# Routed experts: results go to token order by indirect stores inside the tile loop, and come back by plain loads

## The reference, cut to what matters

```
shared = geglu(xf, w1s, w2s, w3s)            # 128 -> 512 -> 128
logits = xf @ Wg                             # 8 experts
idx = argmax(logits, axis=-1)
for e in range(8):
    y = geglu(xf, W1[e], W2[e], W3[e])
    final = final + where(idx == e, y, 0)
x = x + shared + final                       # xf is the normed x
```

## Time and profile before

| | us |
|---|---|
| median of 3 runs | 2236.22 |
| the runs | 2234.86 to 2237.25 |
| span of the profiled execution | 2237.5 |
| the part of the last stage from its first instruction to the start of the routed loop | 1998.7 to 2068.7 |
| routed loop | 2068.7 to 2181.8 |
| last two shared blocks on PE | 2181.8 to 2202.9 |
| after PE's last product | 2202.9 to 2237.5 |

### The profile page before, as it was taken

How to read it: one execution, slowest core, us unless ns; L and a number is a source line. 1 busy time by engine, 2 the same in 40 slices (tenths; PEclk the granted TensorE clock), 3 DMA queues, 4 the chain that set the end, 5 groups by cost and what they waited for, 6 DMA issues and landing times. The chain is left out here.

```text
span 2237.5 us, 80353 instructions
## 1 busy us (share of the span) xinstructions
PE 2061.6 (92%) x27341; PEld 1519.6 (68%) x27342; DVE 1563.5 (70%) x5619; ACT 1272.5 (57%) x3620; POOL 1097.6 (49%) x1151
## 2 busy tenths in 40 slices
PE   7899999988999899988999999999789999989993
PEld 5577777765767677766777777777456666665992
DVE  6878888865777743347999899989666666653542
ACT  5555565556888433336777777777545555532330
POOL 2233434434888200007777777777266666615115
PEclk9999999998999899998999999999899999979997
DMA  6610000000000000001111111111310000001112
GB/s 217 201 64 0 0 0 0 0 1 1 0 0 0 1 1 0 0 9 43 37 35 35 35 35 41 41 35 57 124 53 0 0 0 0 0 2 43 46 41 77
DMA packets 42521, 71.61 MB, mean 32 GB/s; under 512 B 6336, under 2 KB 30912, under 8 KB 41792
## 3 DMA queue, kind: packets, MB, share of 16 engines
q1 hardware_dynamic: 39104, 63.63, 9.0%
q0 software_dynamic: 3328, 6.82, 0.9%
HBM read 61.00 MB, written 9.44 MB: 31 GB/s over the span
## 5 line engine op out<-in xcount | busy, mean ns | idle before, releaser
L2334 ACT ACTIVATE xat_scores<-xat_scores,xat_least 128x257 f32<-128x257 f32 x512 | 258.5, 505 | 83.8 <-DVE xat_least L2475 83.6
L2475 DVE CUSTOM_DVE_ANT_0 xat_scores<-bank,xat_mask_b 128x257 f32<-128x257 f32 x512 | 203.1, 420 | 51.5 <-PE bank L2180 44.9
L1111 POOL TENSOR_TENSOR gqa_rnorm<-gqa_norm_min,gqa_minus_half 128x12 f32<-128x12 f32 x64 | 145.8, 2278 | 103.7 <-DVE gqa_norm_min L1188 103.7
L2236 PE MATMUL bank<-ident,xat_scores 128*128 128x128 f32 x1024 | 189.5, 288 | 0.2 <-DVE xat_p_T L2482 0.2
L751 POOL TENSOR_TENSOR lin_q_softmax<-lin_q_exp,lin_q_rsum 128x512 f32<-128x512 f32 x64 | 66.7, 1042 | 225.2 <-DVE lin_q_rsum L812 225.2
L2236 PEld LDWEIGHTS bank<-ident,xat_scores 128*128 128x128 f32 x1024 | 116.0, 141 | 81.9 <-issue 43.6
L1754 DVE SCALAR_TENSOR_TENSOR X<-bank,expert_shares,X 128x128 f32 (+1 forms) x256 | 72.2, 344 | 130.7 <-PE bank L1668 130.4
L1691 ACT ACTIVATE moe_gelu<-bank 128x512 f32<-128x512 f32 x128 | 76.4, 598 | 146.0 <-PE bank L1658 146.0
L1429 POOL TENSOR_TENSOR bat_scores<-bat_scores,bat_max 128x512 f32<-128x512 f32 x128 | 130.4, 1041 | 32.6 <-DVE bat_max L1461 32.6
L1668 PEld LDWEIGHTS bank<-moe_w,moe_gelu 128*128 128x128 f32 x1024 | 124.2, 192 | 30.8 <-issue 18.4
L1461 DVE CUSTOM_DVE_ANT_0 bat_scores<-bank,bat_causal_add 128x128 f32<-128x128 f32 x512 | 110.7, 286 | 47.0 <-PE bank L1317 47.0
(11 more groups left out here) (325 smaller groups left out, 5891.7 us busy)
## 6 DMA issues: line engine op xcount, KB each, us to landing
glu_ctx_N<-in_ctxN SPq DMA_DIRECT2D x32, 576.0 KB, 3.7
xat_ctx_T<-in_ctxT SPq DMA_DIRECT2D x32, 516.0 KB, 3.6
xat_pad<-in_xat_pad SPq DMA_DIRECT2D x32, 128.5 KB, 3.3
expert_w<-in_glx_w SPq DMA_DIRECT2D x1, 4096.0 KB, 14.6
slot_rows<-gqa_zero_rows SPq DMA_DIRECT2D x1, 2560.0 KB, 11.0
slt_rows<-slot_rows SPq DMA_DIRECT2D x40, 64.0 KB, 1.8
slot_results<-slt_y POOLq DMA_DIRECT2D x40, 64.0 KB, 1.8
moe_w<-in_moe_w SPq DMA_DIRECT2D x2, 1024.0 KB, 5.9
```

Of the source, the lines that this page charges most:

```text
L1111: pool.tensor_tensor(rn[h][:, :], sm[h][:, :], half_neg[:, :], ALU.pow).then_inc(rnorm, 1)
L2236: m = pe.transpose(dst[:, c * P:(c + 1) * P], sx[j % 2][:, g, c * P:(c + 1) * P], k.ident[:, :])
L2334: act.activation(sx[j % 2][:, g, :], sx[j % 2][:, g, :], ACT.Exp, bias=mn[j % 2][g][:, 0:1], scale=-1.0, accum_out=sm[j % 2][:, g:g + 1]). ...
L2475: dve.tensor_tensor_reduce(sx[j % 2][:, g, :], pS[g][:, 0:J], mb[slot][:, j, :], 1.0, BIG, ALU.add, ALU.min, mn[j % 2][g][:, 0:1]).then_in ...
```

## The change

- Each normed row in DRAM gets a 129th word that holds the token's number as an unsigned integer. POOL copies the numbers of all tokens into the last column of `k.XN`; the rows of `slot_rows` are 129 words (516 bytes) now, and so are the scatters and the tile loads. The numbers (`token_numbers`, partition times 32 plus tile) are a new input, loaded with the other weights of the last stage.
- `slot_rows` is no longer filled from a tile of zeros: SP copies it from a new input in DRAM (`empty_rows`), whose rows are zeros and a number beyond 4095, a different one for each slot. POOL's `memset` of the zero tile goes.
- In the routed loop POOL's store of `yo` becomes an indirect store to the row that the 129th word of `xr` names, in a buffer `token_results` of 4096 + 5120 rows. An empty slot's row goes to its own row behind the tokens.
- `xr` must keep the numbers until that store is done. So SP waits for the store before it reloads the buffer, and there are 6 buffers in place of 4.
- The 32 gathers are gone. SP waits for the last stores and issues five plain loads (L1839 of the changed kernel) into a new tile `res`, 4096 or 2048 bytes for each partition.
- DVE adds the first four groups behind the four gates of the last shared block, and only the fifth behind the last add of the shared layer. The output stores follow as before.

```diff
-    WAYS = 4
+    WAYS = 6
...
+            def again(before, t, w, stores):
+                sp.wait_ge(turned, before + 1)
+                sp.wait_ge(stored[w % 2], stores)
+                load(t, w)
+            TURNS = ST // WAYS - 1
+            with sp.Fori(0, TURNS) as i:
                 for w in range(WAYS):
-                    sp.wait_ge(turned, WAYS * i + w + 1)
-                    load(WAYS * i + w + WAYS, w)
+                    again(WAYS * i + w, WAYS * i + w + WAYS, w, 16 * (WAYS // 2 * i + w // 2 + 1))
+            for t in range(WAYS * (TURNS + 1), ST):
+                again(t - WAYS, t, t % WAYS, 16 * ((t - WAYS) // 2 + 1))
+            for w in range(2):
+                sp.wait_ge(stored[w], 8 * ST)
+            of_tokens = results[0:NT * P, :].rearrange("(p t) d -> p t d", t=NT)
+            for g, (lo, hi) in enumerate(GROUPS):
+                sp.dma_start(res[:, lo:hi, :], of_tokens[:, lo:hi, :]).then_inc(gathered[g], 16)
...
+            pool.tensor_copy(k.XN[:, :, D:D + 1].bitcast(U32), tokens[:, :].unsqueeze(2)).then_inc(numbered, 1)
+            pool.wait_ge(numbered, 1)
             pool.wait_ge(slots_known, 1)
             for t in range(NT):
                 pool.indirect_dma_start(rows, bass.IndirectOffsetOnAxis(k.SLOT[:, t:t + 1], 0), k.XN[:, t, :],
                                         None).then_inc(scattered, 16)
-            pool.wait_ge(scattered, 16 * NT)
-            with pool.Fori(0, ST // 2) as i:
-                for w in range(2):
-                    wait_apart(pool, y_copied, 2 * i + w + 1)
-                    pool.dma_start(results[ts(2 * i + w, P), :], yo[w][:, :]).then_inc(stored[w], 16)
-            pool.wait_ge(stored[0], 8 * ST)
-            pool.wait_ge(stored[1], 8 * ST)
-            for g, (lo, hi) in enumerate(GROUPS):
-                for t in range(lo, hi):
-                    pool.indirect_dma_start(k.XN[:, t, :], None, results,
-                                            bass.IndirectOffsetOnAxis(k.SLOT[:, t:t + 1], 0)).then_inc(gathered[g], 16)
+
+            def body(t, slot, first, last):
+                pool.wait_ge(y_copied, t + 1)
+                pool.sem_inc(pool_waited, 1)
+                pool.indirect_dma_start(results, bass.IndirectOffsetOnAxis(xr[slot][:, D:D + 1].bitcast(U32), 0),
+                                        yo[slot % 2][:, :], None).then_inc(stored[slot % 2], 16)
+            steps(pool, ST, body, WAYS)
...
             def sum_results(g, lo, hi):
-                dve.wait_ge(gathered[g], 16 * (hi - lo))
+                dve.wait_ge(gathered[g], 16)
                 dve.wait_ge(added, hi)
-                dve.tensor_tensor(k.X[:, lo:hi, :], k.X[:, lo:hi, :], k.XN[:, lo:hi, :], ALU.add).then_inc(summed, 1)
+                dve.tensor_tensor(k.X[:, lo:hi, :], k.X[:, lo:hi, :], res[:, lo:hi, :], ALU.add).then_inc(summed, 1)
...
                     if c == 1 and b > FIRST:
                         add(b - 1)
+                    if b == NB - 1:
+                        sum_results(c, *GROUPS[c])
             add(NB - 1)
-            for g, (lo, hi) in enumerate(GROUPS):
-                sum_results(g, lo, hi)
+            sum_results(NF, *GROUPS[NF])
...
-            sp.dma_start(slots.rearrange("(m p) d -> p m d", p=P),
-                         zero[:, :].unsqueeze(1).broadcast_to([P, ST, D])).then_inc(cleared, 16)
+            sp.dma_start(slots, empty).then_inc(cleared, 16)
...
+    o["token_numbers"] = (row[:, None] * NT + np.arange(NT)[None]).astype(np.uint32)
+    empty = np.zeros((ST * P, D + 1), np.float32)
+    empty.view(np.uint32)[:, D] = NT * P + np.arange(ST * P)
+    o["empty_rows"] = empty
```

More of the change, by code:

```diff
@@ L819, in _, with stage_clamped_attention @@
             steps(dve, NT, body)
-def stage_clamped_attention(nc, k, w_q, w_kv, wo, gam, nw, mask, slots, ahead):
+def stage_clamped_attention(nc, k, w_q, w_kv, wo, gam, nw, mask, empty, slots, ahead):
     H, DH = 8, 64
@@ L881, in stage_clamped_attention @@
         pe_waited = sem("pe_waited")
-        zero = sb("zero_rows", [P, D])
-        zero_set, cleared = sem("zero_set"), sem("slots_cleared")
+        cleared = sem("slots_cleared")
         ctx.callback(leave_stale, k, sems, scope)
@@ L1099, in body @@
                 if first:
-                    pool.memset(zero[:, :], 0.0).then_inc(zero_set, 1)
                     for i in range(4):
@@ L1229, in _ @@
                 wait(pe, copied, t - 2)
-                pe.transpose(pT[t % 3][:, 0:P], rows[:, t, :], k.ident[:, :]).then_inc(turned, 1)
+                pe.transpose(pT[t % 3][:, 0:P], rows[:, t, 0:D], k.ident[:, :]).then_inc(turned, 1)
                 if wr is not None and t >= 2:
@@ L1249, in _ @@
             for t in range(NT):
-                dve.tensor_scalar(rows[:, t, :], src[:, t, :], k.MV[:, t, 0:1], rstd[:, t:t + 1],
+                dve.tensor_scalar(rows[:, t, 0:D], src[:, t, :], k.MV[:, t, 0:1], rstd[:, t:t + 1],
                                   ALU.subtract, ALU.mult).then_inc(normed, 1)
@@ L1762, in _, with stage_routed_experts @@
             blocks(dve, body)
-def stage_routed_experts(nc, k, low, down, at, shared, w12, w3, rows, results, out):
+def stage_routed_experts(nc, k, low, down, at, shared, w12, w3, tokens, rows, results, out):
     E, F = 8, 512
@@ L1794, in stage_routed_experts @@
         sg = [sb(f"glx_gh{i}", [P, TB * P]) for i in range(2)]
-        xr = [sb(f"slt_rows{i}", [P, D]) for i in range(WAYS)]
+        xr = [sb(f"slt_rows{i}", [P, D + 1]) for i in range(WAYS)]
+        res = sb("results_by_token", [P, NT, D])
         xT = [sb(f"slt_xT{i}", [P, P]) for i in range(2)]
@@ L1808, in stage_routed_experts @@
         scattered, summed, kept = sem("rows_scattered"), sem("results_added"), sem("out_stored")
-        gathered = [sem(f"gathered{g}") for g in range(len(GROUPS))]
+        numbered, pool_waited = sem("rows_numbered"), sem("pool_waited")
+        gathered = [sem(f"results_landed{g}") for g in range(len(GROUPS))]
         landed = [sem(f"rows_landed{i}") for i in range(WAYS)]
@@ L1883, in transpose @@
                 wait(pe, xt_ready, t - 1)
-                pe.transpose(pT[slot % 2][:, 0:P], xr[slot][:, :], k.ident[:, :]).then_inc(turned, 1)
+                pe.transpose(pT[slot % 2][:, 0:P], xr[slot][:, 0:D], k.ident[:, :]).then_inc(turned, 1)
             def h(t, slot):
@@ L2644, in build @@
         counts, router = sb("counts", [P, ST]), sb("glx_router", [P, 8])
+        tokens = sb("token_numbers", [P, NT], U32)
         w12, w3 = sb("expert_w12", [P, 16, 512]), sb("expert_w3", [P, 8 * 512])
         shared = [sb("shared_w1", [P, 512]), sb("shared_w2", [P, 512]), sb("shared_w3", [P, 4, D])]
-        for_last = [(counts[:, :], a["counts"]), (router[:, :], a["glx_router"]),
+        for_last = [(counts[:, :], a["counts"]), (tokens[:, :], a["token_numbers"]), (router[:, :], a["glx_router"]),
                     (shared[0][:, :], a["glx_shared1"][0]), (shared[1][:, :], a["glx_shared2"][0]),
@@ L2651, in build @@
         deviation_phase(nc, k, "ln5", rms=True)
-        stage_clamped_attention(nc, k, *gqa, a["slot_rows"], for_last)
-        k.LT, k.XN = sb("ln6_T", [P, NT, P]), sb("rows_normed", [P, NT, D])
+        stage_clamped_attention(nc, k, *gqa, a["empty_rows"], a["slot_rows"], for_last)
+        k.LT, k.XN = sb("ln6_T", [P, NT, P]), sb("rows_normed", [P, NT, D + 1])
         deviation_phase(nc, k, "ln6")
         stage_norm_transpose(nc, k, "ln6a", k.X, k.XN, wr=router)
-        stage_routed_experts(nc, k, low, down, counts, shared, w12, w3, a["slot_rows"], a["slot_results"], out)
+        stage_routed_experts(nc, k, low, down, counts, shared, w12, w3, tokens, a["slot_rows"], a["token_results"], out)
         with nc.Block() as block:
@@ L2747 @@
     out = nc.dram_tensor("out_0", (B, S, D), F32, kind="ExternalOutput").ap()
-    for name in ("slot_rows", "slot_results"):
-        a[name] = nc.dram_tensor(name, (ST * P, D), F32, kind="Internal").ap()
+    for name, shape in (("slot_rows", (ST * P, D + 1)), ("token_results", (NT * P + ST * P, D))):
+        a[name] = nc.dram_tensor(name, shape, F32, kind="Internal").ap()
     build(nc, a, out)
```

2 lines of the change are left out of this document (removed).

## The result

The changed kernel takes 2210.19 us (median of 4 runs, 2208.85 to 2215.03) against 2236.73 us for the kernel before: a ratio of 0.9879, 95% interval 0.9863 to 0.9896, so 26.5 us less. In two later series it took 2209.52 against 2237.01 and 2211.13 against 2238.05 us, 27.5 and 26.9 us less. The forecast was 2212.0 with a range of 2209 to 2217.

What follows compares the result with a forecast made beforehand. PE bounds the routed loop, POOL's issue of 32 gathers the end. The tail saves 24.4 us, less 0.2 for closer output stores, all else costs nothing: 2236.22 - 24.2 = 2212.0 us, range 2209 to 2217.

Steps and rivals of the forecast that it cites:

- The tail's term: Behind the loop: without gathers, DVE's last sum ends at 2204.4 instead of 2228.78, 24.4 us less.
- Stores to loads: Tail: the last result store lands 2.2 us later, so SP issues the five loads from 2185.0 on.
- The second gap between gates: DVE in the last shared block: the second sum fits before the next gate with only 0.1 us to spare.
- Behind it everything stays, 8.7 us: After DVE's last sum: the last output store and the program's closing take 8.7 us as before.
- The stores in the loop: Routed loop: indirect stores keep POOL 0.96 us instead of 0.54 and cost nothing; at the slowest landing, 2.9 us.
- rival 3: Routed loop: ACT waits for slow store landings, deciding from 4.65 us; 2243 us at a 6.3 us landing; chance 0.05.
- The new wait and its buffers: Routed loop: SP's wait before reloading costs nothing with six buffers, 13.3 us against 16.7; four give only 11.2.
- 13.3 us over four tiles: Routed loop: a buffer's round, from a tile's transpose through products, copy and store to its reload, was put at 13.3 us.
- Long rows: Scatters and tile loads with 516-byte rows: taken at the lower end, as now, since bytes differ by 1%.
- Rival 2: Scatters before the loop keep POOL twice as long; time within 0.2% of the kernel before; chance 0.05.
- The cover: Loop entry: first tile lands at 2059.1, PE wants it at 2068.70, so 9.6 us of scatter delay are hidden.
- Rival 1: Tail: loads finishing together or output stores queueing give back 3.2 us, 2215.2 us; chance 0.10.

Runs made afterwards that it cites:

- late gather: The changed kernel with one indirect POOL gather of 128 rows, read by nobody, after DVE's fourth sum: 2216.35 us.

## Why the prediction was right

- **What bounds.** Right: the chain through POOL's gathers ended the program, and with it gone PE's last product, one add and one sum do.
- **The tail's term**, 24.4 us: 24.3 measured in the profiles from the stage's begin to the last sum. Stores to loads: 2.3 us from the last store's issue to the first load's, 2.2 expected. All landed by 2193.3, with the bound at 2194.1. The second gap between gates had 0.19 us left, 0.1 expected.
- **"Behind it everything stays, 8.7 us"** was the step that failed. Of these 8.7 us SP spent 4.0 waiting for POOL's drain behind its last gather, and 3.6 went with the gathers. With them the sum would have been 27.8 us and the forecast 2208.4, against 2210.2, 2209.5 and 2211.1 in three series. That lies below the stated range: the medians gained less than the profiled executions' 27.9 us, and the number came out within 1.8 us partly because of that. That part is luck. The wait was to be seen in the list of SP's waits, under the wrong engine's name.
- **The stores in the loop**, nothing: right, shown twice (217.5 against 217.7 us, and twice the stores for 0.2 us in the profile). Their landing was 2.2 us, 3.5 at most; rival 3 began at 4.65. A store beside a copy lost 0.36 us at most, where up to 0.69 was allowed.
- **The new wait and its buffers**: that four are too few was right; that they would cost by "13.3 us over four tiles" was not, 5.2 us a tile instead of 3.3, by PE's waits in the round and by the clock (1.7 us for two tiles).
- **Long rows**: right at the lower end, 958 ns a scatter as before. Rival 2, to which 0.05 went, had each scatter keep POOL for twice as long; no run shows that. The cover was 7.4 us and not 9.6.
- **Rival 1**: with the sums behind the last add the output stores do queue, 1.5 us at the median; between the gates they don't (3.2 us at the median, 3.3 before), and the 0.2 us set aside for it weren't needed. The gathers beside which a store landed in 3.3 us were not in its queue: q0 of the page of before moved 6.82 MB, which is POOL's 104 scatters, stores and gathers of 64 KB.

## What to carry to other kernels

A results chain that starts with the last tile of a loop could be hidden here because it was made of few large transfers (five loads, all landed 9.5 us behind the first issue, where the issue of the gathers had taken 40.24 us) and because other work stands behind the loop (21.1 us): move the indexing into the loop, where POOL has time (busy for 20.78 of 113.10 us before, 36.60 after), and put what remains between instructions that have gaps. When a store must read what a load brought, count the buffers by the time from a tile's last use to the next landing against the work in between, not by the round. And before a tail is taken as fixed, look at each engine's drain where the block is left: in the kernel before POOL's ended 8.6 us behind the last instruction that a busy view shows of it, and SP waited 4.0 us for it.

## What the runs showed of the hardware

- POOL's drain ended long after the last of its own DMA issues: 8.6 us after 32 gathers (before), 7.9 after a single one (late gather), 5.9 after the indirect stores (changed kernel), 9.2 after twice as many of them, and 7.4 after plain stores in the kernel without gathers. What sets the time between these wasn't tried. In blocks where POOL issued no DMA its drain took 1.6 us at most. ACT's, PE's and DVE's drains took 0.6, 1.2 and 0.7 us in the changed kernel's last stage.
- An indirect DMA of 128 rows kept POOL for 0.96 us, whether it scattered rows of 512 bytes (before) or of 516 (changed kernel). In the run that stores each result twice, beside a DVE copy of 0.69 us that started after it, it depended on the distance: from 0.30 to 0.50 us (22 pairs) the DMA was held until 0.12 us behind the copy's end, from 0.51 to 0.70 (8) the copy was held, by up to 0.25 us, from 0.77 to 0.89 (6) neither.
- With four buffers 17 waits of 2.0 to 2.9 us on PE, one every 10.3 us, were each followed by 4.6 us at a mean granted clock of 0.63; behind one of them 16 products took 3.65 us in place of 1.95. An earlier wait of 2.77 us was not: the clock stayed at 1.00. In that loop the clock cost 29 us beside 49.4 us of waits. With five shared blocks a stretch of 3.4 us at 0.50 stood behind PE's gap of 3.4 us at the loop's start and cost 1.7 us.
